# A two-layer block with causal attention: weighted sums of two steps issued in one block on TensorE

## The reference, cut to what matters

```
scores = q @ k.T / sqrt(8)                 # per head
layer 0: scores = -inf where key > query   # causal, 1024 keys
layer 1: scores += -1e9 where 3 * key > query (about)   # 342 keys, made by a strided convolution
o = softmax(scores) @ v
```

## Time and profile before

| | |
|---|---|
| median of 3 executions | 1394.3 us |
| the profiled execution, its own time | 1396.07 us |
| its span, first to last instruction | 1394.1 us |
| TensorE busy | 1173.7 us, 84% |
| VectorE busy | 1038.0 us, 74% |
| ScalarE busy | 736.4 us, 53% |
| GpSimd busy | 568.6 us, 41% |
| mean granted clock of TensorE | 0.916 of full speed |

### The profile page before, as it was taken

How to read it: one execution, slowest core, us unless ns; L and a number is a source line. 1 busy time by engine, 2 the same in 40 slices (tenths; PEclk the granted TensorE clock), 3 DMA queues, 4 the chain that set the end, 5 groups by cost and what they waited for, 6 DMA issues and landing times. The chain is left out here.

```text
span 1394.1 us, 28169 instructions
## 1 busy us (share of the span) xinstructions
PE 1173.7 (84%) x8802; PEld 647.6 (46%) x8802; DVE 1038.0 (74%) x2140; ACT 736.4 (53%) x1105; POOL 568.6 (41%) x821
## 2 busy tenths in 40 slices
PE   0655666899989998999999767599999978999993
PEld 0333555344434443444443345345445437888872
DVE  5996998888868886888785154477778736777788
ACT  0552222066656665666567533136566566777772
POOL 5455222023323331333222155336667662466663
PEclk9877998599999999999999877569999999999997
DMA  3343770001221211121100013112222106577541
GB/s 99 94 125 99 127 94 0 16 9 60 97 71 47 70 63 56 47 70 63 40 2 3 1 53 95 37 47 60 60 56 65 43 21 198 182 233 222 190 121 61
DMA packets 98605, 107.93 MB, mean 77 GB/s; under 512 B 16225, under 2 KB 76454, under 8 KB 98480
## 3 DMA queue, kind: packets, MB, share of 16 engines
q1 hardware_dynamic: 93488, 97.83, 25.4%
q0 software_dynamic: 4992, 8.48, 1.8%
HBM read 64.67 MB, written 42.63 MB: 77 GB/s over the span
## 5 line engine op out<-in xcount | busy, mean ns | idle before, releaser
L1105 ACT ACTIVATE a_probs<-a_pst 128x1024 f32<-128x1024 f32 (+4 forms) x544 | 431.9, 813 | 276.1 <-PE a_pst L1035 262.2
L1130 DVE TENSOR_REDUCE a_tops<-a_ps 128x1 f32<-128x512 f32 (+9 forms) x624 | 357.3, 592 | 82.4 <-PE a_ps L1004 69.8
L946 POOL TENSOR_SCALAR_AFFINE_SELECT a_probs<-a_probs 128x256 f32<-128x256 f32 (+3 forms) x384 | 183.0, 483 | 451.1 <-ACT a_probs L1105 448.4
L1004 PE MATMUL a_ps<-kp,qp 96*128 96x512 bf16 (+9 forms) x1280 | 322.7, 312 | 8.3 <-issue 6.3
L1035 PE MATMUL a_pst<-qp,kp 99*128 99x512 bf16 (+4 forms) x1088 | 268.2, 332 | 4.3 <-ACT a_probs L1105 3.2
L1058 PE MATMUL a_po<-a_probs,vh 128*32 128x256 f32 (+2 forms) x3584 | 268.8, 373 | 2.9 <-POOL a_probs L946 1.5
L1130 DVE TENSOR_REDUCE a_tops_lead<-a_ps 128x1 f32<-128x512 f32 x256 | 171.1, 688 | 33.6 <-PE a_ps L1004 31.1
L1004 PEld LDWEIGHTS a_ps<-kp,qp 96*128 96x128 bf16 x1280 | 114.9, 102 | 100.5 <-DVE a_tops_lead L1130 32.0
L1001 PE MATMUL a_ps<-mask_s,identb 128*128 128x128 bf16 (+8 forms) x624 | 148.3, 239 | 9.6 <-PEq L1218 4.5
L1001 PEld LDWEIGHTS a_ps<-mask_s,identb 128*128 128x128 bf16 x624 | 60.6, 98 | 149.7 <-DVE a_tops L1130 55.8
L1676 POOL DMA_INDIRECT chosen_rows<-e_slot_y,e_slot_x x92 | 94.5, 1028 | 86.8 <-DVE e_slot_y L1864 64.8
(11 more groups left out here) (262 smaller groups left out, 1797.2 us busy)
## 6 DMA issues: line engine op xcount, KB each, us to landing
e_slot_w<-weight_parts SPq DMA_DIRECT2D x23, 1024.0 KB
weight_parts<-a_cut SPq DMA_DIRECT2D x18, 512.0 KB, 4.1
k_parts<-o SPq DMA_DIRECT2D x48, 128.0 KB
qp<-q_parts SPq DMA_DIRECT2D x64, 96.0 KB
kp<-k_parts SPq DMA_DIRECT2D x32, 192.0 KB
slot_rows<-empty_row SPq DMA_DIRECT2D x4, 1495.0 KB, 25.0
e_slot_x<-slot_rows SPq DMA_DIRECT2D x23, 260.0 KB
a_raw<-in_wraw SPq DMA_DIRECT2D x18, 256.0 KB, 4.1
```

Source lines behind the costliest of these rows:

```text
L946: pool.affine_select(out=seen, in_=seen, compare_op=ALU.is_ge, fill=0.0, base=m0, pattern=[[0, 2], [1, mw]], channel_multiplier=-1 if laye ...
L1004: last = pe.matmul(bank[:, i * room:i * room + w], sb["qp"][slot][0:KROWS, j, f["qt"] * P:(f["qt"] + 1) * P], sb["kp"][slot][0:KROWS, j // ...
L1105: act.activation(probs[local % RING][0:st["rows"], 2 * part:2 * part + 2, st["off"]:CHUNK], p_st[part][0:st["rows"], :, st["off"]:CHUNK], ...
L1130: dve.tensor_reduce(out, scores, AX.X, ALU.max).then_inc(s["banks_read"], 1)
```

## The change

The weighted sum of a step is no longer cut in halves: it is four matmuls over all its columns. And it no longer follows two steps behind in every step: when three steps are waiting, the weighted sums of the two oldest (n-3 and n-2) are put behind pair a of step n, so in every second step. The buffers `probs` stay 4 (BEHIND + TOGETHER), the score banks stay 3. Fills are still spread by `now`, so they can fall between the two weighted sums, but no longer inside one. The diff is whole.

```diff
--- before.py
+++ after.py
@@ -59,6 +59,7 @@
 BANKS = 3
 BANK_USES = ("fill", "turn_max", "turn_out")
 BEHIND = 2
+TOGETHER = 2
 FIXED = 48
 
 
@@ -737,10 +738,6 @@
 
         return 2 * (CHUNK - st["off"] + FIXED)
 
-    def halves(self, st):
-
-        return [(st["off"], CHUNK)] if st["off"] >= CHUNK // 2 else [(st["off"], CHUNK // 2), (CHUNK // 2, CHUNK)]
-
     def batch_schedule(self, first, last):
 
 
@@ -758,16 +755,14 @@
             out.append((now, entry))
             now += cost
 
-        def weigh(step, half):
+        def weigh(step):
 
             g, n = step
             st = self.steps[n]
-            halves = self.halves(st)
-            if half < len(halves):
-                put(4 * (halves[half][1] - halves[half][0] + FIXED), "weigh", g, n, half)
-                if st["last"] and half == len(halves) - 1:
-                    put(0, "end", g, st["c"], 0)
-                    out.append((now + self.out_time, ("turn_out", g, st["c"], 0)))
+            put(4 * (CHUNK - st["off"] + FIXED), "weigh", g, n, 0)
+            if st["last"]:
+                put(0, "end", g, st["c"], 0)
+                out.append((now + self.out_time, ("turn_out", g, st["c"], 0)))
 
         before = []
         for g in range(GROUPS):
@@ -775,14 +770,15 @@
             for n, st in enumerate(self.steps):
                 for pair in range(2):
                     put(self.pair_cost(st), "pair", g, n, pair)
-                    if len(before) == BEHIND:
-                        weigh(before[0], pair)
-                before = before[-(BEHIND - 1):] + [(g, n)] if BEHIND > 1 else [(g, n)]
+                    if len(before) == BEHIND + TOGETHER - 1:
+                        for step in before[:TOGETHER]:
+                            weigh(step)
+                        before = before[TOGETHER:]
+                before.append((g, n))
             put(0, "next_load", g, 0, 0)
         starts.append(now)
         for step in before:
-            for half in range(2):
-                weigh(step, half)
+            weigh(step)
         starts.append(now + now / GROUPS)
         cost = [len(f["heads"]) * f["width"] + FIXED for f in self.fills]
         for g in range(1, GROUPS if last else GROUPS + 2):
@@ -824,7 +820,7 @@
         def sem(name):
             return ctx.enter_context(nc.semaphore(f"a{layer}_{name}"))
 
-        RING = BEHIND + 2
+        RING = BEHIND + TOGETHER
         probs = [tmp(f"probs{i}", [P, GH, CHUNK]) for i in range(RING)]
         tops = [tmp(f"tops{i}", [P, GH, T // P]) for i in range(2)]
         tops_lead = [tmp(f"tops_lead{i}", [P, GH, T // P - CT]) for i in range(2)]
@@ -1039,28 +1035,24 @@
                                      start=True, stop=True)
                 last.then_inc(s["scores_t_ready"], 1)
 
-            def weigh(b, g, k, half, local):
+            def weigh(b, g, k, local):
 
                 st = geo.steps[k]
                 n = b * GROUPS + g
-                if half == 0:
-                    if k == 0:
-                        pe.wait_ge(s["v_staged"], since["v_staged"] + VS * (n + 1))
-                    if st["first"]:
-                        pe.wait_ge(s["o_copied"], since["o_copied"] + 2 * n + st["c"])
-                    pe.wait_ge(s["exp_done"], since["exp_done"] + 2 * (b * GROUPS * S + local + 1))
-                    if st["mask"]:
-                        pe.wait_ge(s["unseen_zeroed"], since["unseen_zeroed"] + 2 * (M * n + geo.masked.index(k) + 1))
-                halves = geo.halves(st)
-                c0, c1 = halves[half]
+                if k == 0:
+                    pe.wait_ge(s["v_staged"], since["v_staged"] + VS * (n + 1))
+                if st["first"]:
+                    pe.wait_ge(s["o_copied"], since["o_copied"] + 2 * n + st["c"])
+                pe.wait_ge(s["exp_done"], since["exp_done"] + 2 * (b * GROUPS * S + local + 1))
+                if st["mask"]:
+                    pe.wait_ge(s["unseen_zeroed"], since["unseen_zeroed"] + 2 * (M * n + geo.masked.index(k) + 1))
                 for j in range(GH):
 
-                    last = pe.matmul(p_o[VW * j:VW * (j + 1), c0:c1], sb["vh"][g % 2][0:st["rows"], st["kt"], j, :],
-                                     probs[local % RING][0:st["rows"], j, c0:c1],
-                                     start=st["first"] and half == 0, stop=st["last"], tile_position=(0, VW * j),
+                    last = pe.matmul(p_o[VW * j:VW * (j + 1), st["off"]:CHUNK], sb["vh"][g % 2][0:st["rows"], st["kt"], j, :],
+                                     probs[local % RING][0:st["rows"], j, st["off"]:CHUNK],
+                                     start=st["first"], stop=st["last"], tile_position=(0, VW * j),
                                      skip_group_check=True)
-                if half == len(halves) - 1:
-                    last.then_inc(s["pv_done"], 1)
+                last.then_inc(s["pv_done"], 1)
 
             def run(b, schedule, last):
                 use = 0
@@ -1070,7 +1062,7 @@
                     if what == "pair":
                         pair(b, g, k, part, g * S + k)
                     if what == "weigh":
-                        weigh(b, g, k, part, g * S + k)
+                        weigh(b, g, k, g * S + k)
                     if what == "turn_max":
                         turn_max(b, b * GROUPS + g, use)
                     if what == "turn_out":
```

## The result

The changed kernel takes **1442.99 us** (median of four executions, 1441.14 to 1450.12) against 1393.95 us for the kernel before, run beside it (1392.29 to 1396.3). The ratio is 1.036 with a 95% interval of 1.0321 to 1.0399: slower by 3.6%. The forecast was 1434 us with a range of 1388 to 1470. The profiled execution has a span of 1439.2 us, 45.1 us more than before.

What follows compares the result with a forecast made beforehand. TensorE was taken to bound the attention. New waits of 23 us in layer 0, 14 in layer 1 and 3 in the last groups, net of savings, gave +40 us: 1434 us, range 1388 to 1470.

Steps and rivals of the forecast that it cites:

- Saving per block: Weighted sums, both layers: each block costs 0.24 us beside its columns; 185 fewer blocks save 44 us.
- New waits of layer 0: Layer 0 groups: 3.46 us of new TensorE waits against 1.92 saved, +1.54 a group, +23 us over 15 groups.
- 1a and 5a: Layer 0, pairs on side a of steps 1 and 5: each waits 0.41 us for the preceding step's exponential.
- Layer 1: Layer 1 groups: 4.74 us of new waits per two groups, +1.86 after what is taken off, +14 us in all.
- Pair 4b and the sum of step 2: Layer 1: pair 4b waits 0.85 us behind copy and exponential; step 2's sum waits 1.1 for ScalarE's copy.
- 0.93 a group, x 15: Layer 1: each of 15 groups loses 0.93 us net, +14 us together.
- the last group: Last group of each layer, without fills: two full steps take 5.1 us instead of 4.4; about +3 us for both layers.
- clock rival: Inside the attention: new waits lower the clock once in each of 30 groups, 84 us more, 1518 us; chance 0.03.
- granted clock unchanged: Sign that the forecast is right: TensorE's granted clock stays as before the change.
- The waits stay hidden: Rival, pairs between two blocks: no new waits show and the 44 us saving remains, 1350 us; chance 0.13.
- Saving and waits cancel: Rival, both layers: only half of the waits come, so no change, 1394 us; chance 0.06.
- The score banks: Rival, bunched fills: three score banks make fills wait for VectorE's reductions, 31 us more, 1466 us; chance 0.12.

Runs made afterwards that it cites:

- e10: Changed kernel's order, but sums above 256 columns cut into two adjacent pieces: 1446.71 us, 1.0401 of the kernel before.
- e2: The change in layer 0 alone, layer 1 as in the kernel before: 1414.07 us, 1.0153 of the kernel before.
- e4: Changed kernel with every exponential over the first half of its columns only: 1394.89 us, 1.003 of the kernel before.
- e4b: Kernel before with every exponential over the first half of its columns only: 1392.19 us, 1.0001 of the unaltered kernel before.
- e7: Changed kernel with layer 0's turned maxima issued later, behind a sum: 1433.31 us, 1.029 of the kernel before.
- e3: The change in layer 1 alone, layer 0 as in the kernel before: 1420.79 us, 1.0208 of the kernel before.
- e5: Changed kernel, but in layer 1 a block's second sum that opens a new query column goes behind pair b: 1431.36 us, 1.0282 of the kernel before.
- e11: Changed kernel with the second of the two sums issued behind pair b instead of both behind pair a: 1426.15 us, 1.0248 of the kernel before.
- e8: Kernel before with halves joined, one whole sum behind pair a of every step, and both layers' turned maxima later: 1363.64 us, 0.9793 of the kernel before.
- e9: Changed kernel with exponentials over half their columns and layer 0's turned maxima issued later: 1389.82 us, 0.9981 of the kernel before.
- e1: Kernel before with halves joined and one whole sum behind pair a of every step: 1368.38 us, 0.9833 of the kernel before.

## Why the forecast held, and where its sum was off

The time rose by 49 us where 40 were forecast. Layer 0 is right nearly term by term; layer 1 is 12 us short, and the range was wide enough to hold that.

**Saving per block: right.** 0.24 us a block gave 1.92 us for a group of layer 0; the sum of 512 columns was put at 0.99 us and occupies 1.00. e10 shows that the price is one of the block's edges.

**New waits of layer 0: right, each in its place.** By the start distances: 1a and 5a 0.41 each (predicted 0.41), 2b 0.63 (0.62), 10b 0.57 (0.58), 7a 0.23 (0.19), 8b 0.13 (0.13), 11a 0.26 (0.36), 3a 0.05 (0.14), the maxima 0.55 and the bank 0.09 (0.52 and 0.10). All waits before pairs make 2.83 us a group, predicted 2.84. A group inside a batch costs 1.34 us more, predicted 1.54. The 0.2 between is mostly the fill behind the turned maxima: it waited 0.27 us a group in the kernel before already, where I had costed the bank's wait as new. From the second to the last turned maxima of the layer the change costs 16.4 us, where 14 distances of 1.54 would make 21.6; the three distances with a batch's end in them grew by only 1.6 together. e2 measured 22 for the layer, predicted 23 and half of the last groups' 3. That the exponentials cause it is shown by e4 against e4b (48 us), and that the maxima's wait is a term of its own by e7 (9.7 us, 0.53 a group).

**Layer 1: the mechanism right, the sum too low.** I predicted 14 us and half of 3; e3 measured 28. Between the first and the last turned maxima it is 19.7 us, and 5.7 behind them. Inside a batch the working holds: 0.64 us a group against a predicted 0.93. There the waits before pairs are 1.42 us (predicted 1.68) and before sums 0.54 (0.70). The waits before fills and maxima fell from 0.51 to nothing and a wait of 0.24 before a pair went with them, where I had credited 0.72; a new one of 0.24 before the turning of the copied sums I had not seen. Pair 4b and the sum of step 2 wait as foreseen (TensorE's timeline, kernel after):

```profile
1015.75 0.29 PE L1000 MATMUL a_ps<-kp,qp 96*128 96x299 bf16 x1
1016.62 0.41 PE L1031 MATMUL a_pst<-qp,kp 99*86 99x256 bf16 x2 [0.58 <-ACT a_probs L1097]
...
1030.67 0.29 PE L1000 MATMUL a_ps<-kp,qp 96*128 96x299 bf16 x1
1031.65 1.07 PE L1051 MATMUL a_po<-a_probs,vh 128*32 128x512 f32 x8 [0.69 <-ACT a_o_raw L1105]
```

The first term that was mis-sized is "0.93 a group, x 15". Seven of the 15 distances between maxima lie inside a batch and cost 4.2 us together. The other eight, next to a batch's end or the layer's start, cost 15.5, where I had taken them as groups like the rest, at 7.4. The second is the last group: 5.7 us behind the maxima, where 1.5 stood. Part of both is the clock. Kernel after, at the batch ends of layer 1, the granted clock third from the right:

```profile
995.00:1005.00 10.00, 7.54 (x68) 3.31 (x67) 5.32 (x14) 4.73 (x7) 4.08 (x8) 1.00 0.14 40
1005.00:1009.00 4.00, 3.72 (x27) 2.28 (x25) 3.67 (x12) 0.67 (x1) 0.00 (x0) 0.60 0.25 70
1060.00:1064.00 4.00, 3.73 (x22) 1.79 (x25) 1.26 (x4) 0.35 (x2) 1.66 (x3) 0.57 0.05 17
1132.00:1140.00 8.00, 7.78 (x39) 3.56 (x39) 3.97 (x8) 5.59 (x7) 5.79 (x8) 0.57 0.08 22
```

The kernel before, at the first of these places:

```profile
970.00:984.00 14.00, 12.29 (x130) 6.22 (x128) 9.45 (x26) 7.12 (x10) 6.58 (x10) 1.00 0.20 54
```

Before, TensorE was busy for 12.3 of 14 us there and the clock stayed at its upper level. Now it was busy for 7.5 of 10 us, and then the clock was at the lower level for part of the next stretch; a pair of 512 columns at 1007.17 occupies 0.86 us instead of 0.43. The three stretches lose at most 0.40 x 4 + 0.43 x 4 + 0.43 x 8 = 6.8 us of columns at the upper level. The kernel before has no such fall between 932 and 1124 us.

e10 shows what the same waits cost without the falls. It has the changed order and only one fall in layer 1, at the first batch end; at the other two the clock stayed at 1.00, and behind the last maxima as well. Busy time by stretch of e10, at the second batch end and in the last group:

```profile
1064.00:1074.00 10.00, 7.54 (x85) 3.81 (x84) 5.32 (x14) 4.72 (x7) 4.04 (x8) 1.00 0.14 41
1167.00:1192.00 25.00, 18.07 (x191) 8.27 (x190) 2.57 (x10) 15.45 (x22) 16.68 (x25) 1.00 0.08 24
```

The turned maxima around the second batch end, e10 and then the kernel after:

```profile
1059.34 0.22 PE L1046 MATMUL a_ps<-identb,a_top_parts 128*96 128x128 bf16 x1
1076.83 0.23 PE L1046 MATMUL a_ps<-identb,a_top_parts 128*96 128x128 bf16 x1 [0.32 <-DVE a_tops L1163]
1091.97 0.22 PE L1046 MATMUL a_ps<-identb,a_top_parts 128*96 128x128 bf16 x1
...
1052.03 0.22 PE L1009 MATMUL a_ps<-identb,a_top_parts 128*96 128x128 bf16 x1
1071.08 0.23 PE L1009 MATMUL a_ps<-identb,a_top_parts 128*96 128x128 bf16 x1 [0.32 <-DVE a_tops L1122]
1086.21 0.22 PE L1009 MATMUL a_ps<-identb,a_top_parts 128*96 128x128 bf16 x1
```

With the clock at 1.00 the two distances are 17.49 and 15.14 us. The kernel before has 16.08 and 13.02 to 13.57 there, so the waits alone cost about 3 us at each batch end. With the falls the kernel after has 17.67 and 15.65, 19.05 and 15.13, 17.48 and 17.18: the three falls cost 0.7, 1.6 and 2.0, together 4.3 of the 15.5 us. The other 11.2 are longer waits, mostly before pairs. In these two distances e10 waits 3.85 us before pairs and 1.36 before sums, and the kernel before 0.58 and nothing. Pairs stand there with no fill between them, as the two full ones of the kernel after from 1055.77 on. From the last maxima to the last turned sums it is 21.34 us before, 24.76 in e10 and 28.35 after, so of 7.0 us there about 3.4 are waits and 3.6 the clock, which the kernel after had at the lower level for part of that stretch:

```profile
1176.00:1204.00 28.00, 17.55 (x77) 7.98 (x78) 7.01 (x10) 9.52 (x15) 15.78 (x17) 0.63 0.33 108
```

Yet the span behind the last maxima is 276.4 us in e10 and 276.2 after, so in e10 the work behind the attention took those 3.6 us back; why is open. So **the clock rival came true in small**: not in each of 30 groups, but at three places where a batch ends and in the last group. The "granted clock unchanged" of the forecast holds inside the groups of both layers and is wrong at these places. The Trainium skill (TensorE: Matmul & The Clock Gate, A second HAM failure mode: psum-queue depth-cycling) tells of short idle times that bring the clock down. At these three places the trace agrees. At the 0.4 to 0.6 us waits inside layer 0's groups it does not, and in e10 the same waits at two batch ends left the clock at 1.00. In layer 1 between 950 us and its last maxima there are three such falls in e3 and four in e7, two each in e4, e5 and e11, one each in e8, e9 and e10, and one each in e2 and e4b, which have this layer in the order of before; e1 has none. So falls are more frequent with the changed order, but neither the order nor these waits settle whether one comes.

**The rivals.** "The waits stay hidden" named the right saving and the wrong place: e1 has it, with a sum in every step. "Saving and waits cancel" needed half of the waits, and nearly all of them came in layer 0. "The score banks" failed as a cause here: the waits before fills fell in layer 0 (0.27 us a group before, 0.08 after). They come back where the other waits are gone, 0.48 in e1 and 0.47 in e9.

**What the experiments' misses say.** e1 by 8 us at least and e4 and e9 by more were expected too fast, in part for one reason: I took a removed wait as gained. When the exponentials no longer hold TensorE up in layer 0, VectorE's reductions, its tail before the maxima or GpSimd's zeroing do, since each has only some tenths of a microsecond to spare. For e4 I also took layer 1's waits too low: 4 us in all for the copy, where sums and turnings wait 0.67 us a group, and nothing around the maxima. Most of what e4 and e9 lack against e1 lies there. e11 was expected too fast since I counted sums that stand together instead of following each pair's buffer. Of the missing 17 us of e1, 10 lie between layer 0's first and last maxima (18.6 us gained, where 15 x 1.92 is 28.8) and 2 between layer 1's; the rest is open.

## What to carry to other kernels

A fixed cost per switch of work on the bound engine is worth removing, and here joining pieces of the same item did it (halves into one sum: 1.7% faster, 2.1% with the turned maxima moved behind a sum); joining different items bunched the others and cost 3.6%. With one PSUM buffer for each pair, the room between a pair and the next use of its buffer must be as long as pair, latency and exponential together (1.71 us here), at every place and not on average: follow each buffer through the new row and compare. Count batch ends, the layer's start and the last group apart from the steady groups: here they cost 21 of layer 1's 25 us, mostly by longer waits and for about a third by the clock. A stretch without the fall, found in another run of the same order, tells the two apart.

## What the runs showed of the hardware that was not expected

- Two adjacent weighted sums of 256 columns occupy 1.00 us, like one of 512, while between other matmuls each occupies 0.57 and 0.10 before it. 176 cuts inside a block cost at most 3.7 us together. The fp32 turning of the copied sums over the whole array has no such edges.
- In the kernel after the granted clock fell at three of the batch ends in layer 1, at the first after a stretch with TensorE busy for 7.54 of 10 us. In e10 the same stretch of the same order (its long sums in two pieces), busy for the same 7.54 us, was followed by a clock of 1.00 at two batch ends. Some eight waits of 0.1 to 0.6 us in each group of layer 0 left it at the upper level.
- In e2 and e4b the groups of layer 1, in the order of before, came 13.25 us apart instead of 13.53: the wait of 0.24 to 0.27 us before a pair of 256 columns, once a group in the kernel before, is missing there. Why is open. Against 13.25 the change costs 0.93 us a group inside a batch, which is what the prediction had.
